# Attention and mixture of experts on one core: the last batch's join is placed in the first mixture's block, and the setup's steps in the last half of attention change order

## The reference

```python
h = _L0_tok_ref(x, L0_tok_W)
h = jnp.concatenate([h, txt], axis=1)
h = h + _L0_attn_ref(_layernorm(h), ...)      # softmax attention, then @ w_out + b_out
h = h + _L0_ffn_ref(_layernorm(h), ...)       # 16 experts, top 2, hidden width 128
h = h + _L1_attn_ref(_layernorm(h), ...)      # a recurrent, linear attention
h = h + _L1_ffn_ref(_layernorm(h), ...)       # 8 experts, top 2, hidden width 256
```

```python
q, k, v = jnp.split(x @ w_qkv + b_qkv, 3, axis=-1)
attn = jax.nn.softmax(jnp.einsum('bhid,bhjd->bhij', q, k) * scale, axis=-1)
out = jnp.einsum('bhij,bhjd->bhid', attn, v)
return out.transpose(0, 2, 1, 3).reshape(b, n, d) @ w_out + b_out
```

```python
topk_vals, topk_idx = jax.lax.top_k(x @ gate_w + gate_b, K)
topk_w = jax.nn.softmax(topk_vals, axis=-1)
h = jax.nn.relu(jnp.einsum('bsh,ehf->bsef', x, w1) + b1)
expert_out = jnp.einsum('bsef,efh->bseh', h, w2) + b2
```

## Time and profile before

| | |
|---|---|
| median of three runs | 2081.71 us |
| the profiled execution | 2085.75 us, of which the span from first to last instruction is 2083.9 us |
| PE busy | 1835.7 us, 88% of the span |
| DVE busy | 1233.1 us, 59% |
| ACT busy | 1046.6 us, 50% |
| POOL busy | 348.4 us, 17% |
| mean granted TensorE clock | 0.922 of full speed |

### The profile page before, as it was taken

One profiled execution on the slowest core, in us unless ns is written; L12 is line 12 of the kernel. 1 busy time (PEld: TensorE's weight loads), 2 busy tenths in 40 slices (PEclk: granted clock), 3 DMA queues, 4 the chain that ended last, 5 costly groups with the idle time before them and its releaser, 6 DMA issues. The chain is left out here.

```text
span 2083.9 us, 41201 instructions
## 1 busy us (share of the span) xinstructions
PE 1835.7 (88%) x15691; PEld 798.1 (38%) x15691; DVE 1233.1 (59%) x3083; ACT 1046.6 (50%) x1967; POOL 348.4 (17%) x330
## 2 busy tenths in 40 slices
PE   6857998989898989899859999998499997999999
PEld 2321222222222222222224444443189884444444
DVE  2448887877786877778514577765536653323321
ACT  1320676767675766667544555544223332555554
POOL 1222000000000000000100246546102343000000
PEclk9975999999998999999989999998769997999999
DMA  5533012111112111201026666440120002332240
GB/s 204 195 73 53 8 29 40 29 40 29 40 28 40 29 40 24 40 13 37 24 56 129 112 130 115 88 86 3 35 56 22 1 2 44 63 78 49 54 83 20
DMA packets 87090, 116.67 MB, mean 56 GB/s; under 512 B 30078, under 2 KB 71128, under 8 KB 84848
## 3 DMA queue, kind: packets, MB, share of 16 engines
q1 hardware_dynamic: 82300, 104.86, 23.9%
q0 software_dynamic: 3104, 8.72, 1.3%
q10 hardware_dynamic: 1492, 0.46, 0.1%
HBM read 95.19 MB, written 18.82 MB: 55 GB/s over the span
## 5 line engine op out<-in xcount | busy, mean ns | idle before, releaser
L795 ACT ACTIVATE b_prob<-b_p_s 128x512 f32<-128x512 f32 x1104 | 571.1, 603 | 347.2 <-PE b_p_s L979 330.6
L818 DVE TENSOR_REDUCE b_m<-b_p_m 128x1 f32<-128x1024 f32 x512 | 603.6, 1219 | 154.2 <-PE b_p_s L979 123.1
L931 PE MATMUL b_p_m<-b_k,b_q 48*64 48x512 bf16 x2048 | 379.3, 425 | 68.7 <-DVE b_m L818 23.2
L979 PE MATMUL b_p_s<-b_q,b_k 51*64 51x512 bf16 x2048 | 362.3, 407 | 8.5 <-ACT b_prob L795 8.0
L1007 PE MATMUL b_p_o<-b_prob,v_all 128*9 128x512 f32 x2304 | 316.4, 633 | 1.0
L931 PEld LDWEIGHTS b_p_m<-b_k,b_q 48*64 48x64 bf16 x2048 | 95.6, 110 | 457.2 <-DVE b_m L818 265.2
L1343 ACT ACTIVATE n_hidden<-n_p_z 128x704 f32<-128x704 f32 x192 | 135.0, 755 | 112.6 <-PE n_p_z L1260 112.6
L1343 ACT ACTIVATE d_hidden<-d_p_z 128x704 f32<-128x704 f32 x192 | 135.0, 755 | 112.0 <-PE d_p_z L1260 112.0
L770 POOL DMA_DIRECT2D sum_scr<-b_sums x48 | 26.3, 548 | 825.1 <-ACT b_sums L785 825.1
L1456 DVE TENSOR_TENSOR d_xg<-d_xd,d_c_wide 128x352 f32<-128x352 f32 x192 | 116.4, 635 | 66.6 <-PE d_p_z L1260 58.4
L1260 PE MATMUL n_p_z<-n_xg,n_w 64*128 64x352 f32 x768 | 142.8, 487 | 0.0
(11 more groups left out here) (332 smaller groups left out, 2151.3 us busy)
## 6 DMA issues: line engine op xcount, KB each, us to landing
d_c_wide<-d_c_scr SPq DMA_DIRECT2D x48, 704.0 KB, 14.2
m_x_all<-n_c_scr SPq DMA_DIRECT2D x48, 352.0 KB, 7.9
xt<-in_x SPq DMA_DIRECT2D x16, 1024.0 KB, 8.6
sum_scr<-b_sums POOLq DMA_DIRECT2D x32, 256.0 KB, 2.7
b_q<-qk_scr SPq DMA_DIRECT2D x96, 66.0 KB
qk_scr<-a_qk_part SPq DMA_DIRECT2D x24, 256.0 KB, 2.8
k_rate<-rate_scr SPq DMA_DIRECT2D x8, 528.0 KB, 4.9
b_k<-qk_scr SPq DMA_DIRECT2D x16, 198.0 KB
```

Source lines behind the costliest of these rows:

```text
L795: nc.scalar.activation(prob[:, U % PR_RING, 0:w], p_s[:, U % S_RING, 0:w], ACT.Exp, scale=float(D) ** -0.5).then_inc(exp_done, 1)
L818: nc.vector.tensor_reduce(m3[:, x, 0:1], p_m[:, s, :, :].rearrange("p k n -> p (k n)"), axis=AX.X, op=ALU.max).then_inc(rows_free, 1)
L931: last = nc.tensor.matmul(out[e:e + 64, k, :], q_st[s][r, i, t * P + e:t * P + e + 64], k_st[s][r, i, k * WIDE:k * WIDE + WIDE], start=Tru ...
L979: last = nc.tensor.matmul(out[e:e + 64, :], k_st[s][r, q, jt * P + e:jt * P + e + 64], q_st[s][r, q, a * WIDE:a * WIDE + WIDE], start=True ...
```

## The change

The six steps of a join become functions of their own at the head of `attend_stage`: `load_sums` and `spread_inverse` (the two halves of `turn_sums`), `invert`, `divide` (`normalise` before), `project` and `add_rows`. They are kept in `own["late"]`, and the tiles that they use are allocated in a context that lives on through the first mixture. For batches 0 to 6 they are called where their work was before. For batch 7 they are called in the first mixture's block: `load_sums` as SP's first step, `spread_inverse` after `spread_in(0, (1, 2))`; `invert` on DVE in group 2; `divide` on POOL after the memset; `project` on PE in group 7 after `turn_gates`, into `p_g` and `p_l`; `add_rows` on DVE in group 7. The semaphore clears move behind the join. In the last half of attention `keep_weights` moves behind `normalise(1)`, and POOL's `rstd_of(0)` and `rstd_of(1)` are placed two sends earlier.

```diff
-        by_itself_at(-2, B - 1, JOIN)
...
-                if p == HG - 1:
-                    turn_sums(sp, b)
+                if p == HG - 1 and b + 1 < B:
+                    load_sums(sp, b)
+                    spread_inverse(sp, b)
...
-                if n == NQ * SUMS - SUMS:
+                if n == NQ * SUMS - SUMS - 2:
                     rstd_of(0)
                     rstd_of(1)
...
-            normalise(B - 1)
...
                 measure(0)
                 gather(0)
-                keep_weights()
                 normalise(0)
                 double(0)
                 measure(1)
                 gather(1)
                 normalise(1)
+                keep_weights()
...
+    INVERT_GROUP, JOIN_GROUP = 2, 7
...
+    if feed:
+        order.append((JOIN_GROUP, 1, "join", B - 1, 0))
...
-        def main():
+        def main(stale):
             nc.gpsimd.memset(own["yT"][:, SEQ:NT * P], 0.0).then_inc(set_up, 1)
+            if feed:
+                divide = own["late"][3]
+                divide(pool, B - 1)
             for it in range(B):
+                if feed and it == 1:
+                    pool.wait_ge(misc_free, join_use() + 1)
+                    for sem in stale:
+                        pool.sem_clear(sem)
...
+        def join_last():
+            project = own["late"][4]
+            pe.wait_ge(misc_free, join_use())
+            project(pe, B - 1, own["p_g"], own["p_l"]).then_inc(misc_full, 1)
...
+                    if feed and i == JOIN_GROUP:
+                        join_last()
                     first(i)
...
+        def join_last():
+            add_rows = own["late"][5]
+            dve.wait_ge(misc_full, join_use() + 1)
+            add_rows(dve, B - 1, own["p_g"][:, :], own["p_l"])
+            dve.sem_inc(misc_free, 1)
...
+                    if feed and i == INVERT_GROUP:
+                        invert = own["late"][2]
+                        invert(dve, B - 1)
+                    if feed and i == JOIN_GROUP:
+                        join_last()
...
+                if feed:
+                    load_sums, spread_inverse = own["late"][0:2]
+                    load_sums(sp, B - 1)
                 spread_in(0, chunks)
+                if feed:
+                    spread_inverse(sp, B - 1)
                 run()
...
-                for sem in stale:
-                    pool.sem_clear(sem)
-                run()
+                run(stale)
```

More of the change, by code:

```diff
@@ L585, in attend_stage, with load_sums @@
         g.sem("c_" + n) for n in ("w_in", "biased", "den_in", "num_in", "inverted", "inv_sent", "inv_in", "att_ready", "joined"))
+    SPAN = SEQ // 16
+    keep = lambda n, s: late_ctx.enter_context(nc.sbuf_tensor(n, s, F32))
+    w_out, den, inv = keep("c_w_out", [P, D]), keep("c_den", [P, SPAN]), keep("c_inv", [P, SPAN])
+    num, inv_wide, attT = keep("c_num", [P, SEQ]), keep("c_inv_wide", [P, SEQ]), keep("c_attT", [P, SEQ])
+    def load_sums(sp, b):
+        e = b % 2
+        for k in range(2):
+            sp.wait_ge(sum_sent[k], 16 * SUMS * (b + 1))
+        rows = g.sum_scr[b, :, :, :].rearrange("p (i r) t -> r (p i) t", r=32)
+        sp.dma_start(den[:, :], rows[DH, :, :].rearrange("h (s n) -> h s n", n=SPAN)).then_inc(den_in, 16)
+        if b >= 2:
+            sp.wait_ge(att_ready, b - 1)
+        sp.dma_start(num[e * D:e * D + D, :], rows[0:DH, :, :].rearrange("d h t -> h d t")).then_inc(num_in, 16)
@@ new lines, in divide, with project @@
+    def divide(pool, b):
+        r = slice(b % 2 * D, b % 2 * D + D)
+        pool.wait_ge(num_in, 16 * (b + 1))
+        pool.wait_ge(inv_in, 16 * (b + 1))
+        if b >= 2:
+            pool.wait_ge(joined, 2 * (b - 1))
+        nc.gpsimd.tensor_tensor(attT[r, :], num[r, :], inv_wide[r, :], ALU.mult).then_inc(att_ready, 1)
+        pool.wait_ge(att_ready, b + 1)
+    def project(pe, b, out, out_text):
+        r = slice(b % 2 * D, b % 2 * D + D)
+        pe.wait_ge(w_in, 48)
+        pe.wait_ge(att_ready, b + 1)
+        for t in range(FULL):
+            nc.tensor.matmul(out[:, t * D:t * D + D], attT[r, t * P:t * P + P], w_out[r, :], start=True, stop=True)
+        return nc.tensor.matmul(out_text[0:TXT, 0:D], attT[r, TOK:SEQ], w_out[r, :], start=True, stop=True)
@@ new lines, in add_rows @@
+    def add_rows(dve, b, out, out_text):
+        dve.wait_ge(biased, B + 1)
+        nc.vector.tensor_tensor(g.hid[:, b, 0:FULL, :].rearrange("p t d -> p (t d)"), g.hid[:, b, 0:FULL, :].rearrange("p t d -> p (t d)"),
+                                out, ALU.add).then_inc(joined, 1)
+        nc.vector.tensor_tensor(g.hid[0:TXT, b, FULL, :], g.hid[0:TXT, b, FULL, :], out_text[0:TXT, 0:D], ALU.add).then_inc(joined, 1)
+        dve.wait_ge(joined, 2 * b + 2)
+    own["late"] = (load_sums, spread_inverse, invert, divide, project, add_rows)
@@ L942, in rows @@
                 if x == JOIN:
[L943 to L946, removed]
+                    last = project(pe, j, out[:, 0, :], out[:, 1, :])
                 elif x < FULL_ROWS:
@@ L1100, in out_use, with join_use @@
         return misc_use["out", b, r]
+    def join_use():
+        return misc_use["join", B - 1, 0]
     def gating(i, k):
@@ L2204, in all_stages @@
         g.swap_sems()
-        attend_stage(g, v_all, own, steps)
+        attend_stage(g, v_all, own, steps, c2)
         g.swap_sems()
```

69 lines of the change are left out of this document (19 added, 50 removed).

## The result

| | before | after |
|---|---|---|
| median of four runs each, taken in turn | 2088.18 us (2078.38 to 2097.87) | 2060.57 us (2057.46 to 2064.66) |
| ratio, with its 95% interval | | 0.9875 (0.9831 to 0.9918) |
| span of the profiled execution | 2083.9 us | 2059.5 us |
| mean granted clock | 0.922 | 0.933 |

The account below looks back on a forecast made before the run. A chain of waits bounds the border, PE the mixture. Border -22.5, setup -7.4, join +7.8 and +0.3 sum to -21.8 us: 2063.9 for the profiled execution, 2060 on the median's scale, range 2051 to 2071.

Parts of the forecast that it names:

- The sum of -21.8 us: Whole kernel: -22.5 - 7.4 + 7.8 + 0.3 us, from the profiled 2085.75 to 2063.9 us, 2059.9 on the median's scale.
- The border: Between attention's last product and the first mixture: PE's first product starts at 1075.3 instead of 1097.81, gaining 22.5 us.
- With 0.4 us for the barrier the mixture begins at 1074.97: At attention's end: the block ends when the last sums have landed, at 1074.57, and the barrier adds 0.4 us.
- the first microseconds run at half clock: Mixture's start: PE at half clock as before; if the clock stays up, some 1.4 us more are gained.
- The clears cost nothing: On POOL behind the join: 5.6 us of semaphore clears, hidden because batch 3's tokens are turned some 35 us later.
- The setup: Last half of attention: DVE prepares the tokens earlier, so PE's stretch takes 7.0 instead of 14.4 us, gaining 7.4.
- Both waits have the same cause and it goes: Last half of attention: reason for taking the full 7.4 us; PE's waits were 2.38 and 3.48 us.
- the setup frees less: Rival, chance 0.20: PE meets the next wait at once; half the gain gives 2063.6 us, none 2067.3.
- The join in group 7: First mixture: PE waits 3.7 us for POOL and joins in 4.1, losing 7.8 us; 0.3 more for group 8.
- Small DMAs that don't wait: Rival, chance 0.15: the inverse lands in a few us, the join costs 2.7 instead of 8.1 us; time 2054.5.
- Chunks that come late: Rival, chance 0.12: group 4's margin of 1.9 us for chunk 1's second load is gone; about 2 us, 2062.
- Slower: Rival, chance 0.03: the join's two dependent DMAs take 20.4 us each, group 7 costs 30.7 us; time 2082.8.

Follow-up runs that it names:

- e5: Changed kernel with the last two sends of partial sums issued by SP instead of POOL; 2058.79 us in one run.
- e4: Changed kernel with 67 of the 76 semaphore clears put back on POOL ahead of the memset; 2057.54 us in one run.
- e2: Kernel before with only the new order of the setup, the join not moved; median 2068.91 us, ratio to before 0.9922.
- e8: Changed kernel with the inverse's two DMAs issued on SP between the loads of chunk 1 and chunk 2; 2055.06 us in one run.
- e9: Changed kernel with the last two sends on SP and the inverse's DMAs between chunk 1 and chunk 2; median 2056.82 us, ratio to before 0.9839.
- e7: Changed kernel with the inverse's two DMAs issued from ACT's queue instead of SP's; 2067.57 us in one run.
- e3: Changed kernel with the old order of the setup, so only the moved join; median 2080.23 us, ratio to before 0.9968.
- e1: Kernel before, unchanged, for a second profile; 2105.35 us in one run.
- e11: Kernel before, unchanged, for a third profile; 2091.54 us.
- e12: Changed kernel with the old order of the setup, so only the moved join, for a second profile; 2080.26 us.

## Why the prediction was right, and where it was not

**The time.** Forecast 2060.0, measured 2060.57 us, and faster by more than 1%. Both hit, but partly by luck, because two things stood against each other. The sum of -21.8 us was made for a profile, and there the touched stretch gave -20.6; that these are so near is luck too, since the border gave 3.9 us less than forecast and the join cost 2.8 us less. It was then set on a median of three runs, 2081.71. Before's median over the sessions is 2088 to 2090, and the gain between the medians 27.6 and 31.3 us. A low start and a small gain made the right end.

**The border, -22.5; measured -18.6.** The step that failed is "With 0.4 us for the barrier the mixture begins at 1074.97". The chain was read well up to POOL's branch (the last send lands, 1073.0 in after), but between a branch and the barrier stands POOL's drain. It was in the trace of before, at the block's end, hidden beside PE's join and DVE's adds; the term was 3.9 us too large for want of it. e5 shows it: with the drain earlier PE's gap is 2.4 us, near the 3.1 forecast. That the first microseconds run at half clock was right (turn of 1.12 us).

**The clears cost nothing: right.** e4 puts a price of 5.0 us on them where they had been; behind the join they delay nothing.

**The setup, -7.4; measured -7.3 between the first profiles, and some 12 us more in most others.** "Both waits have the same cause and it goes" holds, and the nine units go a little faster than forecast (1028.87 to 1034.83 is 6.0 us, 7.0 forecast). What was mis-sized is the clock: the term took over how soon it came back in the one profile. Three of the five profiles with the waits lose 12 us more from A to B, one 21. e2 alone, with 16 us by the ratio and 20.8 between the medians, shows that this is the change's real size. The rival that the setup frees less (0.20) was wrong in its direction.

**The join in group 7, +7.8 and +0.3; measured +5.3 together.** The mechanism was right: the inverse waits behind the loads (11.2 us; forecast "some 14"), POOL is late and PE waits for it. The size was off twice. POOL is ready 26.6 us after the first product, not 27.8, and PE gets there at 24.8 and not 24.1, so the wait is 1.78 and not 3.7 us. And after 1.78 us the join's 18 instructions still run at full clock, 2.2 and not 4.1 us. With 3.46 us of wait (e5) they take 3.5, most of them at half clock as forecast. The turn of group 8 waits 1.25 us, 0.6 more than before, where 0.3 were added. 1.8 + 2.2 + 0.6 is 4.6; the last 0.7 us is the slower way to the join.

**The other rivals.** Small DMAs that don't wait: wrong, 11.2 us, and 8.7 us on the other queue. Chunks that come late: DVE waits 3.95 us for the first of chunk 1's tiles in after, but that far ahead of PE that PE doesn't wait; in e8, with chunk 2 issued later, D to F is 26.1 us as in after. Slower: the spread took 4.2 us, as forecast and not 20.

**Still open.** Why the clock comes back after 10 us in one execution and after 35 or 65 in another, with the same instructions and nearly the same waits (3.5, 4.6 and 3.7 us before the second turn), no run here tells. Nor does one tell what sets the length of POOL's drain. Nor is e9's gain on the median settled.

## What to carry to other kernels

Before taking work out of a block's tail, read the rows of the block's end on each engine: what was hidden there (here a drain of 4 us on POOL) is the next bound, and the engine that must leave last should be one that drains quickly. A wait of 2 to 5 us on PE can cost more than its own length, because here the clock stayed at half for tens of microseconds of full work afterwards in four profiles of five; price it from several executions, since one profile may show the lucky case. And a small DMA that others wait for should be issued ahead of the large loads: another queue brought nothing here (e7), as the DMA engines were occupied.

## What the runs showed of the hardware

- POOL's drain at the end of the attention block took 3.99 us in after, e3, e4 and e8 and 3.82 us in e5; in these PE's took 0.33, ACT's 0.21, SP's 0.12 or less. At the ends of the other blocks of after POOL's took 0.04 to 2.29 us, so the 4 us are this block's.
- Clearing a semaphore on POOL took 75 ns (5.0 us for 67 in e4).
- PE's clock stayed at 0.50 for 30 to 65 us with PE busy nearly throughout (e1, e3, e11, e12), and after one and the same wait of 1.03 us it fell in some executions and stayed at 1.00 in others.
- 33 KB landed in 2.4 us alone, 4.7 behind 1.4 MB, 11.2 behind 2.8 MB on the same queue (e8, after), and 8.7 beside them on another (e7).
